# Triangular systems of a delta-rule layer, split in three groups with memory of their own and solved two rows at a time

## The reference, cut to what matters

```
k = x / max(norm(x), 1e-12)              # per head of 128
v = (x @ W_write.T) * beta ; k_beta = k * beta        # beta = sigmoid(x @ W_beta.T)
A0 = tril(-(k_beta @ k.T * L), -1)       # L: decay by distance of tokens
A  = solve_triangular(I - A0, I, lower=True, unit_diagonal=True)
v  = A @ v
o  = tril(k @ k.T * L) @ v               # the state is zero in the only chunk
h  = h + out + o @ W_read.T              # out = layernorm(h)
logits = layernorm(h) @ Wr + br          # then the best of 8 experts for each token
```

## Time and profile before

| | us |
|---|---|
| median of 3 runs | 834.07 (833.72 to 834.9) |
| profiled execution | 836.92 |
| its span | 835.1 |
| PE busy | 678.3 (81%) |
| DVE busy | 448.1 (54%) |
| POOL busy | 260.3 (31%) |
| ACT busy | 229.1 (27%) |

### The profile page before, as it was taken

The page is one execution under the profiler, slowest core; times in us unless marked ns, Lnnn a source line. Parts: engine busy times, 40 slices in busy tenths (PEclk is TensorE's granted clock), DMA queues, the critical chain, the costliest instruction groups (busy, mean ns, idle before and its releaser), DMA issues. The chain is left out here.

```text
span 835.1 us, 13690 instructions
## 1 busy us (share of the span) xinstructions
PE 678.3 (81%) x4562; PEld 519.5 (62%) x4562; DVE 448.1 (54%) x1266; ACT 229.1 (27%) x635; POOL 260.3 (31%) x418
## 2 busy tenths in 40 slices
PE   5899999999977149999983385196569999999994
PEld 4567677777755139999972364085436767667673
DVE  1567777777765742444799199466613333333321
ACT  0223333333322043443431022032013232232321
POOL 2344444444441012455453122022012221222211
PEclk9899999999986558999997589578569999999998
DMA  8211111111000000000100670193411111111110
GB/s 303 93 35 34 34 35 34 34 35 33 2 2 1 0 2 0 7 7 6 25 7 4 171 303 1 27 356 96 196 50 39 57 47 50 57 44 52 51 32 20
DMA packets 24643, 49.77 MB, mean 60 GB/s; under 512 B 15284, under 2 KB 15414, under 8 KB 23936
## 3 DMA queue, kind: packets, MB, share of 16 engines
q1 hardware_dynamic: 20960, 34.43, 12.7%
q0 software_dynamic: 3328, 10.23, 4.0%
q10 hardware_dynamic: 288, 4.25, 1.3%
HBM read 39.03 MB, written 9.86 MB: 59 GB/s over the span
## 5 line engine op out<-in xcount | busy, mean ns | idle before, releaser
L1762 PE MATMUL psum<-arena_w,work 128*128 x208 | 95.9, 605 | 1.0 <-DVE work L1814 1.0
L1860 ACT ACTIVATE work<-psum,cst 128x128 f32<-128x128 f32 x208 | 56.6, 383 | 144.1 <-PE psum L1775 144.1
L1786 PE MATMUL psum<-arena_w,work 128*128 x416 | 94.2, 379 | 0.4 <-ACT work L1860 0.4
L1786 PEld LDWEIGHTS psum<-arena_w,work 128*128 128x128 f32 x416 | 77.1, 190 | 10.5 <-issue 1.1
L1724 POOL DMA_INDIRECT out<-work,row_i x26 | 25.8, 990 | 160.2 <-DVE work L1836 160.2
L1823 DVE COPY work<-psum 128x512 f32<-128x512 f32 x52 | 36.0, 692 | 70.0 <-PE psum L1762 61.9
L346 PE MATMUL psum<-arena_w 128*111 128x256 f32 x264 | 64.1, 396 | 4.9 <-DMA arena_w<-in_pack 4.9
L1762 PEld LDWEIGHTS psum<-arena_w,work 128*128 128x128 f32 x208 | 38.3, 194 | 40.1 <-issue 40.1
L711 POOL TENSOR_TENSOR arena_w<-arena_w,work 101x592 f32<-101x592 f32 x33 | 39.6, 1200 | 72.2 <-DVE work L577 72.2
L346 PEld LDWEIGHTS psum<-arena_w 128*111 128x111 f32 x264 | 46.5, 183 | 19.7 <-issue 9.6
L1130 PE MATMUL psum<-tokens,work 111*111 111x128 f32 x88 | 18.2, 340 | 43.4 <-POOL work L1537 43.4
(11 more groups left out here) (216 smaller groups left out, 1344.6 us busy)
## 6 DMA issues: line engine op xcount, KB each, us to landing
arena_w<-in_w SPq DMA_DIRECT2D x2, 4096.0 KB, 13.3
arena_w<-in_x SPq DMA_DIRECT2D x22, 333.0 KB, 2.9
x_rows<-tokens SPq DMA_DIRECT2D x22, 192.0 KB, 5.7
arena_w<-in_pack ACTq DMA_DIRECT2D x1, 2420.0 KB, 10.9
cst<-in_packc ACTq DMA_DIRECT2D x1, 1727.0 KB, 14.9
arena_w<-in_pack SPq DMA_DIRECT2D x1, 818.5 KB, 7.3
arena_w<-in_pack SPq DMA_DIRECT2D x2, 384.0 KB, 4.6
work<-a_rows SPq DMA_DIRECT2D x21, 32.4 KB, 2.0
```

Source lines behind the costliest of these rows:

```text
L1762: mm = nc.tensor.matmul(bank[2 * j + f][:, :], xgt[j][:, k * 128:(k + 1) * 128], arena_w1[:, bass.ds(expert * (2 * FF) + (k * FF + f * 512 ...
L1786: mm = nc.tensor.matmul(bank[7][:, 0:D], ht[j][:, g * 128:(g + 1) * 128], arena_w2[:, bass.ds(expert * (FC * D) + g * D, D)], start=(g == ...
L1860: nc.scalar.activation(ht[j][:, g * 128:(g + 1) * 128], bank[4 + f][:, k * 128:(k + 1) * 128], ACT.Gelu, bias=cst[:, bass.ds(expert * FC + ...
```

## The change

Three groups instead of two: pairs 0 to 4, 5 to 7, 8 to 10, with 2, 3 and 4 sets on 120, 108 and 128 partitions. Each has its own system and inverse (`place_of`): the old place, the region of parameters no longer used, and the region of the first products' input. So no group waits for another's place; substitutions stand in a queue, and `advance` carries over from one to the next. SP stores and loads group 0's inverses between the stores of tiles 18 and 19.

A step covers rows i and i + 1. For this the odd rows' links to their predecessor are multiplied into the even rows beforehand (two passes of 648 elements). Products carry one dimension more (2 rows, columns, j). The start of the inverse, an identity, is made by comparing column numbers, once per group.

Strengths are multiplied in by POOL after folding, so that DVE masks both heads in one instruction. In the tile loop ACT normalises with scale and bias, for which POOL makes the product of mean and power, one tile later than before; so the loop is one turn longer.

```diff
-CUTS = [i if i < 8 else 6 if i < 18 else 16 for i in range(TOK)]
 MT = 19
 RL = 112
-GROUPS = ((0, 6), (6, PAIRS))
-SLOTS = (1.0, 1.0, 5.0, 1.7)
+GROUPS = ((0, 5), (5, 8), (8, PAIRS))
+SETS = [128 // (2 * (min(B, 6 * p1) - 6 * p0)) for p0, p1 in GROUPS]
+COLS = [-(-TOK // sets) for sets in SETS]
+SLOTS = (0.7, 0.8, 4.2, 0.6)
...
-            ac = wc(NT * H1 * TOK, RL)
+            prod = [wc(2 * 16 * TOK), wc(2 * 21 * 11)]
...
+            ac = arena_w2[0:RL, W2S // 2 + NT * H1 * R:W2S // 2 + NT * H1 * (R + TOK)]
...
-                stride = 32 * -(-H1 * nb // 32)
-                return im0, im1, nb, stride, 128 // stride
+                return im0, im1, im1 - im0, H1 * (im1 - im0), SETS[g]
+
+            def place_of(g):
+
+                if g == 0:
+                    return sys_n, sys_x[:, 0:TOK * COLS[0]]
+                arena = arena_w2 if g == LAST else arena_w1
+                return arena[:, 0:TOK * TOK], arena[:, TOK * TOK:TOK * (TOK + COLS[g])]
...
-                    sp.wait_ge(cleared, 1)
-                    if g:
-                        sp.wait_ge(solved[g - 1], 1)
+                    if g == LAST:
+                        sp.wait_ge(z1_done, PAIRS)
...
-                    if g:
-                        store_inverses(g - 1)
+                        if t == NT - NB and g == LAST > 0:
+                            store_inverses(0)
+                            load_inverses(0)
                     load_systems(g)
-                for g in range(LAST):
+                for g in range(1, LAST):
+                    store_inverses(g)
...
-                for t in range(NT + 3):
+                for t in range(NT + 4):
                     solve_values(t)
                     read_out(t - 1)
-                    turn_outputs(t - 3)
+                    turn_outputs(t - 4)
                     attend(t)
-                    router_logits(t - 3)
+                    router_logits(t - 4)
...
+                def normalise_outputs(t):
+                    if not tile(t):
+                        return
+                    act.wait_ge(powered2, t + 1)
+                    nc.scalar.activation(x_half(t), h_rows(t), ACT.Identity, bias=ve2[t % 2][:, 2:3],
+                                         scale=ve2[t % 2][:, 1:2]).then_inc(normed2, 1)
...
+                    normalise_outputs(t - 3)
                     copy_solved(t)
-                    copy_turned(t - 3)
+                    copy_turned(t - 4)
...
-                    dve.wait_ge(strong, t + 1)
                     free(dve, nk_ready, t - 1)
-                    for h in range(H1):
-                        cols = slice(h * R, (h + 1) * R)
-                        last = nc.vector.scalar_tensor_tensor(nf[t % 2][:, cols], bank[7][0:R, cols],
-                                                              strength[:, t * H1 + h:t * H1 + h + 1], ln[:, cols],
-                                                              ALU.mult, ALU.mult)
-                    last.then_inc(n_masked, 1)
+                    nc.vector.tensor_tensor(nf[t % 2], bank[7][0:R, 0:H1 * R], ln, ALU.mult).then_inc(n_masked, 1)
+
+                def identity_columns(g):
+
+                    at_col = sum(COLS[:g])
+                    used, cols = group_of(g)[3] * SETS[g], COLS[g]
+                    shape = [used, cols, TOK]
+                    if g == LAST:
+                        dve.wait_ge(z1_done, PAIRS)
+                    nc.vector.tensor_tensor(place_of(g)[1][0:used, :].rearrange("p (c i) -> p c i", c=cols),
+                                            c("lane", used)[:, 0:TOK].unsqueeze(1).broadcast_to(shape),
+                                            p2("col_no", used)[:, at_col:at_col + cols].unsqueeze(2).broadcast_to(shape),
+                                            ALU.is_equal).then_inc(zeroed[g], 1)
...
+                    links = rows_n[0:used, 2 * TOK + 1:TOK * TOK:2 * TOK + 2]
+                    nc.vector.tensor_tensor(spare, n[:, 1::2, 0:TOK - 1], links.unsqueeze(2).broadcast_to([used, half, TOK - 1]),
+                                            ALU.mult).then_inc(paired[g], 1)
+                    dve.wait_ge(paired[g], 1)
+                    nc.vector.tensor_tensor(n[:, 2::2, 0:TOK - 1], n[:, 2::2, 0:TOK - 1], spare, ALU.add).then_inc(paired[g], 1)
+                    dve.wait_ge(paired[g], 2)
+                    nc.vector.memset(rows_n[0:used, 0:TOK * TOK:TOK + 1], 1.0).then_inc(diagonal[g], 1)
+                    dve.wait_ge(diagonal[g], 1)
                     dve.wait_ge(zeroed[g], 1)
-                    for s in range(sets):
-                        own = len(range(s, TOK, sets))
-                        end = 128 if s == sets - 1 else (s + 1) * stride
-                        first = nc.vector.memset(sys_x[s * stride:end, s:s + (own - 1) * (TOK + sets) + 1:TOK + sets], 1.0)
-                        first.then_inc(zeroed[g], 1)
-                    dve.wait_ge(zeroed[g], 1 + sets)
-                    dve.wait_ge(n_in[g], 16 * H1 * sets)
-                    if sets > 1:
-                        nc.vector.memset(sys_n[0:used, 0:TOK * TOK:TOK + 1], 1.0).then_inc(diagonal[g], 1)
-                        dve.wait_ge(diagonal[g], 1)
-                    yield 1.5
-                    last_cut = 0
-                    for i in range(1, TOK):
-                        cut = CUTS[i] // sets if CUTS[i] < i else i
-                        if cut != last_cut:
-                            for which in range(2):
-                                free(dve, chain[which], steps[which])
-                            last_cut = cut
-                        most = -(-i // sets)
-                        end = i + (sets > 1)
-                        parts = [(0, 0, min(cut, most))]
-                        if cut < most:
-                            parts.append((1, cut, most))
+                    yield 2.2
...
+                    for i in range(1, TOK, 2):
+                        most = (i + 1) // sets + 1
+                        parts = [(0, 0, min(split, most))]
+                        if split < most:
+                            parts.append((1, split, most))
                         cost = 0.0
                         products = []
                         for which, c0, c1 in parts:
                             j0 = c0 * sets
-                            w = prod[which][:, 0:(c1 - c0) * (end - j0)].rearrange("p (c j) -> p c j", c=c1 - c0)
+                            shape = [used, 2, c1 - c0, i + 2 - j0]
+                            w = prod[which][0:used, 0:2 * shape[2] * shape[3]].rearrange(
+                                "p (r c j) -> p r c j", r=2, c=shape[2])
                             products.append(w)
                             free(dve, chain[which], steps[which])
-                            nc.vector.tensor_tensor(w, x[:, c0:c1, j0:end],
-                                                    n[:, i, j0:end].unsqueeze(1).broadcast_to([used, c1 - c0, end - j0]),
+                            nc.vector.tensor_tensor(w, x[:, c0:c1, j0:i + 2].unsqueeze(1).broadcast_to(shape),
+                                                    n[:, i:i + 2, j0:i + 2].unsqueeze(2).broadcast_to(shape),
                                                     ALU.mult).then_inc(chain[which], 1)
                             steps[which] += 1
-                            cost += 2 * (0.16 + (c1 - c0) * (end - j0) / 960)
+                            cost += 2 * (0.15 + 2 * shape[2] * shape[3] * 0.0012)
                         for (which, c0, c1), w in zip(parts, products):
                             dve.wait_ge(chain[which], steps[which])
-                            nc.vector.tensor_reduce(x[:, c0:c1, i], w, AX_X, ALU.add).then_inc(chain[which], 1)
+                            nc.vector.tensor_reduce(x[:, c0:c1, i:i + 2].rearrange("p c r -> p r c"), w, AX_X,
+                                                    ALU.add).then_inc(chain[which], 1)
                             steps[which] += 1
                         yield cost
...
+                def advance(budget, most=0):
+
+                    while len(queue) > most and budget > 0:
+                        cost = next(queue[0], None)
                         if cost is None:
-                            pending[0] = None
+                            queue.pop(0)
                         else:
                             budget -= cost
...
                     advance(SLOTS[0])
-                    if i - 2 in ends:
-                        advance(math.inf)
                     decay_products(i - 2, 0)
                     add_outputs(i - 1)
                     advance(SLOTS[1])
                     normalise(i - 1)
                     decay_products(i - 2, 1)
-                    if i - 2 not in ends:
-                        advance(SLOTS[2])
-                    elif ends[i - 2] < LAST:
-                        pending[0] = substitution(ends[i - 2])
-                advance(math.inf)
```

(40 more changed lines are left out.)

54 lines of the change are left out of this document (21 added, 33 removed).

## The result

| | before | after |
|---|---|---|
| median, 4 runs each | 834.49 us | 810.13 us (808.64 to 810.74) |
| profiled execution (span) | 836.92 (835.1) | 810.74 (808.9) |

The account below looks back on a forecast made before the run. DVE's substitution was taken to end both PE halts, each followed by a trip through memory. Terms from pair loop to tail put the end at about 557 against 582, 25 us gained: median 834.07 to 809, range 794 to 820.

Parts of the forecast that it names:

- price of a step: DVE's substitution: 1.05 ns per element and pass, plus 0.44 us fixed for a step of one part, 0.25 for two.
- Rival D: Substitution products in three free dimensions run at half rate, 33.6 us more, none hidden: 843 us, slower; chance 0.05.
- Pair loop: DVE sets the pace from iteration 7; last masking at 457 against 463.2, bounds 451 to 461.
- POOL's collisions: Tile loop: POOL and DVE get in each other's way, 0.2 us a tile, 2.8 us in all.
- Start of the tile loop: PE starts at 458.6 instead of 473.54, after the last fold (0.95) and the spreading (0.6): 15 us, the largest term.
- Second update: Second row update of the tile loop waits for group 2's loads and starts at 471.5; without the wait 468.
- Rival B: Second halt at the tile loop's start, group 0's inverses late or DVE over by more: 10 us, 819; chance 0.12.
- Tile loop: From second update to last inverse: updates 27.2, substitution 13.8, collisions 2.8, slow PE 3; sum 46.8, solved at 518.3.
- The hole: Before tile 16 PE waits for the last group's inverses: 7.5 us store, 2.4, hand-off 0.2; tile 16 at 528.4.
- The tail: From tile 21 at 546.7, 10 us to the end; SP's backlog of rows just hidden, 5 us if not.
- C: PE stays at 1.2 GHz through the tile loop: 7 us gained, 827 us; chance 0.06.
- A: DVE not held by loads, clock stays at 2.4 GHz, engines do not collide: 38 us gained, 796; chance 0.22.

Follow-up runs that it names:

- late-preparation kernel: Changed kernel, in which a new group leaves one place of DVE's order empty before it waits for its systems; 798.61 us, ratio 0.9527.
- store-early kernel: Changed kernel with SP storing group 0's inverses behind tile 16 instead of 18, their load left behind tile 18; 804.9 us, ratio 0.9631.
- kernel with all three edits: Changed kernel with group 0's store behind tile 16, a place left empty ahead of each group, and tile-iteration budget 1.7 instead of 0.6; 790.96 us.
- last experiment: Kernel with all three edits, plus SP writing the rows of tiles 0 to 9 before it stores the last group's inverses; 787.91 us, ratio 0.9437.
- budget cut: Changed kernel's substitution budget of 0.6 in a tile iteration; undone to 1.7, as before the change, the changed kernel took 796.75 us, ratio 0.9543.

## Why the prediction was right

**Right: price of a step.** The step of 592 + 462 products with three free dimensions took from 427.36 to 429.82, 2.46 us; 0.25 + 2,108 x 0.00105 is 2.46 (2,108 is 1,054 products, multiplied and summed). Rival D falls with it.

**Pair loop: mechanism right, size short by 3 to 5 us.** Iterations 7 to 11 took 17.1, 11.9, 13.7, 16.1 us, then 14.3 to the last masking, against 15.3, 11.7, 13.2, 14.8 and 13.5. The wait terms were 3.19 and 4.03 us instead of 2.2 and 2.6. These make 2.4 of the 4.6 us too little. The late-preparation kernel has neither wait, and its loop is 8.9 us shorter, 7.2 of it the waits themselves. The rest fits steps that met POOL: 90 products took 0.77 us and 132 products 0.41 (rows above), where the sums over the same products took 0.25 and 0.29. Up to the last masking eight of 34 steps show this, POOL busy at each, 3.4 us together, while the other multiplications lie within 0.03 us of their sums. That covers the 2.2 us left; it was not tried by itself. The prediction put POOL's collisions on the tile loop only.

**Start of the tile loop: the step that failed most, 5.1 us.** Of it 3.2 come from the masking's end. The other 1.9 lie behind it: 1.55 us were put for the last fold and the spreading, and 3.5 passed. POOL's timeline from 459.88, and DVE's beside it:

```profile
459.88 0.19 POOL L1522 TENSOR_SCALAR arena_w<-arena_w 111x2 f32<-111x2 f32 x1
460.15 0.92 POOL L1523 TENSOR_TENSOR arena_w<-arena_w 111x2 f32<-111x2 f32 x1
461.15 0.19 POOL L1524 TENSOR_TENSOR arena_w<-arena_w 111x2 f32<-111x2 f32 x1
```
```profile
460.16 0.86 DVE L1401 TENSOR_TENSOR work<-arena_w 108x350 f32<-108x350 f32 x2
```

An operation of two elements took 0.92 us and ended with DVE's multiplication (461.07 and 461.02). POOL was not done with its small operations when the masking was, and each could be held by a step of DVE. In the late-preparation kernel, where the longest of the four took 0.46 us instead of 0.92, the way is 2.7 us. That POOL's work costs nothing until the last tile was true; the price of the last tile was not.

The Trainium skill (SBUF — State Buffer, the term "shared port pair") has one of the two block for the whole instruction of the other. Here the trace agrees with that rule: 0.92 us for two elements, up to the end of DVE's multiplication, where the prediction had kept to 0.4 us.

**Second update: the wait for loads was forecast, but from a wrong store time.** The store of group 0 was put at 446 and stood at 449.82, as its last steps ran late with the loop; its trip took 7.79 us, not 7.0. So SP was held until 462.93 instead of 459, and the loads of group 2 landed some 4 us late (473.46 against 469.5). DVE still stood only 2.48 us for them and not 3.6, as the first update came late too. This is a part of rival B, SP waiting in order, at another place and with a smaller price: the store-early kernel gets back 2.5 us at the second update and 5 to 7 us in all. Rival B's halt as such (first spreading waiting for its load) did not come: it waited for the fold.

**Tile loop: 46.8 us put, 42.2 taken** (475.41 to the last sum's end at 517.6). The cold PE (3 put) is there: DVE waited 2.8 us for it, in two pieces, at the slow tiles. That leaves 39.4 for row updates and steps, which were priced at 27.2 + 13.8 = 41.0, so nothing is left on DVE for the collisions (2.8 put): no multiplication of a step took over 0.46 us (29 instructions, up to 296 products each). The collisions fell on POOL instead. Its power of one element met DVE's step in each tile and grew with it, from 0.55 to 1.02 us, 2.7 us over ten tiles (POOL's timeline, and the step beside it):

```profile
513.11 1.02 POOL L1559 TENSOR_TENSOR work<-work 111x1 f32<-111x1 f32 x1 [1.14 <-DVE work L1445]
...
525.19 0.55 POOL L1559 TENSOR_TENSOR work<-work 111x1 f32<-111x1 f32 x1
```
```profile
513.02 0.71 DVE L1401 TENSOR_TENSOR work<-arena_w 128x280 f32<-128x280 f32 x2
```

DVE did not wait for POOL there, so it cost nothing. The spreading, which had held a step before, lay beside the row update and took 0.56 us, and the update 1.00, as alone. Where it did meet a step, in the kernel that normalises on DVE (at 489.25, 0.69 us), the step's multiplications took 0.74 us and their sums 0.34. So none of the 16 us that the same skill rule gave for this stretch show on DVE, because of what lay beside what; that the update reads one input from PSUM may be why it was not held, which no run tests.

**The hole: 10.1 us put from solved to tile 16, 7.7 taken.** The trip was 5.03 us instead of 7.5. The trips go with the number of pieces of 148 bytes: 2,220, 1,332 and 1,184 pieces took 7.8, 5.4 and 5.0 us here, and in the other kernels 7.6 to 8.4, 4.6 to 6.0 and 5.0 to 6.1. The prediction gave 7.5 for 1,184 pieces on the ground of more issues, though its own row had 7.0 for 2,072. Tiles 16 to 21 took 18.45 us, as forecast (18.3).

**The tail: the cover was gone.** "Just hidden, at 5 us if it is not": SP wrote rows until 554.12, and the phase began 3.5 us behind the last logits, 1.7 before. That is 1.8 us; in the kernel with all three edits it is 6.7, and the last experiment shows the cause.

**The other rivals.** C, PE at 1.2 GHz through the loop, did not come: in the tile loop the clock was low only in the first tiles and behind the two halts. A, more gained, named three savings (no wait for loads, full clock, no collision); the third came in the tile loop alone. Updates stood 2.5 to 3.1 us apart from the sixth on, not 2.9 to 3.4.

So the sum came out by terms that cancelled: 5.1 us too little at the start, then 1.2 too much up to the second update, 4.6 in the loop, 2.4 in the trip and 0.5 in the tail. That it met the median within 1.1 us is in good part luck. Main terms (start, hole, six tiles instead of ten) were the right ones, at other sizes: 9.8 us were gained at the start (15 forecast), 15.3 by the first tile behind the hole (12.2), and 27.4 by the last (24.5), as only six tiles were left behind it. Undone singly, two rows a step are worth 12 to 13 us, memory of its own some 4 to 6 (not clear by time alone), ACT's part 4, and the strengths nothing that shows. These 20 to 23 us beside 24.4 need not add up, since the budget cut costs 12 to 14 by itself; three groups instead of two were not tried alone.

## What to carry to other kernels

Time a hand-off by the consumer's place in its own queue: work that an engine reaches just behind the last producer step stands for the whole trip of store and load, and moving it by one place in the code gained some 14 us here. When work moves into an earlier stage, set the later stage's budgets anew; a lower one alone cost 12 to 14 us. Behind the last producer, count the other engine's small operations too, at the price they have beside the first engine's multiplications.

## What the runs showed of the hardware

- A multiplication on DVE with two inputs from SBUF and an operation of POOL held one another: on POOL 0.92 us for two elements at 460.15 and 1.41 us at 455.65, where 0.19 to 0.20 us are usual; on DVE 0.77 us for 90 products at 398.38, where 88 took 0.25 at 442.46. These ended at 399.15, POOL's instruction, which had begun at 397.95, at 399.04.
- PE ran at half clock behind a short halt too: behind 1.56 us (last kernel) four matmuls took 1.19 us and the tile 4.12, while 0.84 us in the kernel with three edits left 0.69 us and 2.59. But 1.41 us earlier in the last kernel (476.90) and 1.54 us in the kernel before (490.30) left 0.69 us too, so the length of the halt alone does not tell. Behind 4.1 to 5.0 us (three kernels) one or two tiles were slow, behind 10.5 to 12.5 us two or three.
- The trip of stores in pieces of 148 bytes went with the number of pieces, not with the number of issues: 7.6 to 8.4 us for 2,220 pieces in 4 issues, 4.6 to 6.0 for 1,332 in 6, 5.0 to 6.1 for 1,184 in 8, over the kernels in which nothing else held the queue.
